# Two gated cross-attention layers on one core: in layer one ScalarE writes the masked keys, and the work of a turn is put in a new order

## The reference

```python
x = x + tanh(g_xattn[0]) * L0_xattn(layernorm(x), ctx, ctx, ...)
x = x + tanh(g_ffn[0])   * L0_ffn(layernorm(x), ...)      # 8 experts, one per token
x = x + tanh(g_xattn[1]) * L1_xattn(layernorm(x), ctx, ctx, pad_mask, ...)
x = x + tanh(g_ffn[1])   * L1_ffn(layernorm(x), ...)      # 16 dense experts

def L0_xattn(query, key, value, ...):                     # 16 heads of 8 dimensions
    q = (query @ Wq + bq).reshape(b, s, 16, 8)
    k = (key @ Wk + bk).reshape(b, s, 16, 8)
    v = (value @ Wv + bv).reshape(b, s, 16, 8)
    scores = einsum('bqhd,bkhd->bhqk', q, k) / sqrt(8)
    scores = where(k_pos < (q_pos // 32 + 1) * 32, scores, -1e9)
    return einsum('bhqk,bkhd->bqhd', softmax(scores), v) @ Wo + bo
```

## Time and profile before

| | us |
|---|---|
| three timed runs | 1631.96, 1639.06, 1639.1 (median 1639.06) |
| the profiled execution | 1626.43 |
| its span, first to last instruction | 1624.7 |
| granted TensorE clock, mean over the span | 0.981 |

### The profile page before, as it was taken

One profiled execution on the slowest core, in us unless ns is written; L12 is line 12 of the kernel. 1 busy time (PEld: TensorE's weight loads), 2 busy tenths in 40 slices (PEclk: granted clock), 3 DMA queues, 4 the chain that ended last, 5 costly groups with the idle time before them and its releaser, 6 DMA issues.

```text
span 1624.7 us, 52801 instructions
## 1 busy us (share of the span) xinstructions
PE 1513.6 (93%) x17129; PEld 1308.8 (81%) x17130; DVE 1293.3 (80%) x4044; ACT 1064.2 (65%) x2661; POOL 1186.9 (73%) x1715
## 2 busy tenths in 40 slices
PE   5899999976999789999999999999999999999996
PEld 4666666755999469888888888888888888889885
DVE  3777778863555378998999889988998999988885
ACT  3777777743556456767766776677667766776664
POOL 4556666642456568888888888888888888888785
PEclk9999999986999999999999999999999999999998
DMA  2322222234553100000000000000000000000000
GB/s 78 110 72 74 78 78 78 78 102 120 147 140 91 29 16 15 20 16 15 21 19 17 15 21 15 21 15 21 15 21 15 17 19 21 15 15 18 5 8 11
DMA packets 92108, 69.05 MB, mean 42 GB/s; under 512 B 13937, under 2 KB 87697, under 8 KB 91921
## 3 DMA queue, kind: packets, MB, share of 16 engines
q1 hardware_dynamic: 76512, 49.34, 10.3%
q0 software_dynamic: 5120, 12.62, 2.4%
q10 hardware_dynamic: 10288, 4.74, 1.1%
HBM read 35.74 MB, written 22.52 MB: 36 GB/s over the span
## 4 chain that ended last, share of the span: by engine, by line
PE 79%; issue 7%; DVE 6%; ACT 3%; DMA 2%; POOL 2%; SPq 1%; POOLq 0%; ACTq 0%; DVEq 0%
PE s_bank L1998 12%; PE s_bank L1999 11%; PE s_bank L2000 11%; PE tb L1815 6%; PE po L1945 4%; PE s_bank L1933 4%; PE s_bank L1795 4%; PE po L1829 3%; PE m L1769 2%; PE s_bank L2146 2%; PE s_bank L1804 2%; ACT pT L889 1%; DVE qkv L1552 1%; DMA kx<-kT 1%; PE s_bank L2133 1%
## 5 line engine op out<-in xcount | busy, mean ns | idle before, releaser
L745 POOL TENSOR_TENSOR qkv<-qkv,scaled 128x384 f32<-128x384 f32 x480 | 489.4, 1020 | 87.2 <-ACT scaled L1020 37.8
L1020 ACT ACTIVATE scaled<-s_bank,wg 128x384 f32<-128x384 f32 x449 | 260.3, 584 | 114.5 <-PE s_bank L2000 109.9
L1998 PE MATMUL s_bank<-proj_hi,hn_hi 128*128 128x384 f32 x900 | 327.0, 363 | 5.6 <-DVE qkv L1552 5.6
L1552 DVE SCALAR_TENSOR_TENSOR qkv<-s_bank,wg,qkv 128x384 f32<-128x384 f32 x449 | 273.9, 610 | 49.8 <-PE s_bank L2000 39.6
L1999 PE MATMUL s_bank<-proj_lo,hn_hi 128*128 128x384 f32 x900 | 302.9, 337 | 0.0
L2000 PE MATMUL s_bank<-proj_hi,hn_lo 128*128 128x384 f32 x900 | 302.2, 336 | 0.0
L889 ACT ACTIVATE pT<-tb 128x512 f32<-128x512 f32 x256 | 152.9, 597 | 136.1 <-PE tb L1815 134.5
L1998 PEld LDWEIGHTS s_bank<-proj_hi,hn_hi 128*128 128x128 f32 x900 | 169.4, 188 | 18.9 <-DVE qkv L1552 14.1
L1815 PE MATMUL tb<-ident,prob 128*128 128x128 f32 x1024 | 161.4, 281 | 15.2 <-ACT pT L889 13.8
L1999 PEld LDWEIGHTS s_bank<-proj_lo,hn_hi 128*128 128x128 f32 x900 | 170.2, 189 | 1.6
L2000 PEld LDWEIGHTS s_bank<-proj_hi,hn_lo 128*128 128x128 f32 x900 | 169.0, 188 | 0.0
(11 more groups left out here) (285 smaller groups left out, 3714.3 us busy)
## 6 DMA issues: line engine op xcount, KB each, us to landing
xs<-sorted_in SPq DMA_DIRECT2D x71, 128.5 KB, 2.1
kx<-kT SPq DMA_DIRECT2D x256, 32.0 KB
sorted_out<-yo SPq DMA_DIRECT2D x71, 64.0 KB, 1.6
xin<-in_x SPq DMA_DIRECT2D x32, 128.0 KB, 2.1
cin<-in_ctx SPq DMA_DIRECT2D x32, 128.0 KB, 2.3
ctx_cols<-xcT SPq DMA_DIRECT2D x32, 128.0 KB, 1.7
w<-in_L_ffn_W SPq DMA_DIRECT2D x16, 256.0 KB, 3.8
xcT<-ctx_cols SPq DMA_DIRECT2D x32, 128.0 KB, 2.8
```

What stands on the lines that cost most here:

```text
L745: g.tensor_tensor(into, into, scaled[m % SCALED][:, 0:cols], ALU.add).then_inc(dense_added, 1)
L1020: ins = act.activation(into, bank[:, 0:3 * D], ACT.Copy, scale=wg[v % 4][:, 1, k:k + 1])
L1552: v.scalar_tensor_tensor(out=acc, in0=bank[:, 0:3 * D], scalar=wg[w % 4][:, 0, k:k + 1], in1=acc, op0=ALU.mult, op1=ALU.add).then_inc(dens ...
L1998: pe.matmul(bank[:, 0:cols], hi[:, tile], of(proj_hi), start=True, stop=False)
```

## The change

- **Masked keys on ScalarE.** `place_keys` and `keys` are no longer used in layer one (layer two keeps them). `head_keys` reads the keys of m1 four times and writes kx[:, r, :] whole, each time with a scale column `head_mask[:, r]` (one in the partitions with p mod 4 = r, zero elsewhere) and a bias column `head_bias[:, r]` (the key bias times that mask). The two columns are made once at the start by VectorE. `k_ready` now counts two a unit, and TensorE's products wait for it in place of `keys_placed`.
- **ScalarE's turn.** exp of quad 0 before the last copy of probabilities; the four key writes and the queries before the copy of x1T; exp of quad 1 behind them; exps in the order 0, 1, 3, 2.
- **VectorE's turn.** `first_rows` a turn earlier, before the last maximum; `router_logits` ahead of `return_heads`; `router_onehot` ahead of `add_residual`; `second_rows` ahead of the first maximum; the second maximum ahead of `router_select`. `output_bias` is prepared one turn earlier.
- **TensorE's turn.** It begins with `scores`; `output(0, u)` closes the turn (the same place as before, since it stood first in the turn after). `router_rank` comes before `transpose_probs` of quad 2, `subtract_max` of quad 0 before `transpose_probs` of quad 3, and `subtract_max` of quad 3 before `transpose_probs` of quad 0.

```diff
+            def head_keys(v, pair):
+                q = s[0]
+                if exists(v):
+                    act.wait_ge(q["qk_in_psum"], v + 1)
+                    wait(act, q["scores_in_psum"], 4 * v)
+                    for r in (2 * pair, 2 * pair + 1):
+                        ins = act.activation(kx[:, r, :], m1[:, 256:512], ACT.Identity,
+                                             bias=head_bias[:, r:r + 1], scale=head_mask[:, r:r + 1])
+                    ins.then_inc(q["k_ready"], 1)
...
             def body0(u, par):
                 q = s[0]
+                exp_quad(q, u + 1, 0)
                 copy_pT(q, u, 3)
-                exp_quad(q, u + 1, 0)
                 apply_second_norm(0, u - 1, lambda t: xr[1 - par][:, t, 0:D], lambda t: xr[1 - par][:, t, D:2 * D])
+                head_keys(u + 2, 1)
+                head_keys(u + 2, 0)
+                queries(0, u + 2)
+                copy_x1T(u - 1)
                 exp_quad(q, u + 1, 1)
-                queries(0, u + 2)
-                keys(0, u + 2)
-                copy_x1T(u - 1)
-                exp_quad(q, u + 1, 2)
                 copy_pT(q, u + 1, 0)
                 exp_quad(q, u + 1, 3)
+                exp_quad(q, u + 1, 2)
                 copy_v(q, u + 2, par)
...
+            v.tensor_reduce(head_mask[:, :], ident[:, :].rearrange("p (m r) -> p r m", r=4), AX_X, ALU.add)
...
+            v.tensor_scalar(head_bias[:, :], head_mask[:, :], bcol[:, 1:2], None, ALU.mult)\
+                .then_inc(setup["first_steps"], 1)
...
                 if exists(u + 2):
                     store_context(u + 2, par)
-                    place_keys(0, u + 2)
...
                     pe.wait_ge(q["qk_ready"], v + 1)
-                    pe.wait_ge(q["keys_placed"], 64 * (v + 1))
+                    if q is s[0]:
+                        pe.wait_ge(q["k_ready"], 2 * v + 2)
+                    else:
+                        pe.wait_ge(q["keys_placed"], 64 * (v + 1))
...
-                output(0, u - 1)
                 scores(0, u + 1, 1 - par)
+                router_rank(u - 2)
                 transpose_probs(q, u, 2)
-                router_rank(u - 2)
                 transpose_in(0, u + 2, par)
+                subtract_max(q, u + 1, 0)
                 transpose_probs(q, u, 3)
-                subtract_max(q, u + 1, 0)
...
                 transpose_probs(q, u + 1, 1)
+                output(0, u)
```

More of the change, by code:

```diff
@@ L33 @@
 LOWER_MAXIMA = (0, 1, 3, 2)
-LOWER_SUBTRACTED = (0, 1, 2, 3)
+LOWER_SUBTRACTED = (0, 1, 3, 2)
 SLOTS = N // P + E0 - 1
@@ L162, in flamingo @@
         kx = sb("kx", [P, 4, UNIT])
+        head_mask = sb("head_mask", [P, 4])
+        head_bias = sb("head_bias", [P, 4])
         vb = [sb(f"vb{b}", [P, 4, 8, 2, VW]) for b in range(2)]
@@ L417, in load_unit, with place_keys @@
                 sp.dma_start(cin[par][:, :, :], tokens(a["ctx_1024"], v)).then_inc(ctx_loaded[0][par], 16)
-            def place_keys(layer, v):
-                q = s[layer]
+            def place_keys(v):
+                q = s[1]
                 sp.wait_ge(q["k_ready"], v + 1)
-                if layer == 1 and v == 1:
+                if v == 1:
                     sp.wait_ge(q["scores_in_psum"], 4)
@@ L512, in _ @@
                 load_slot(sl, sl, rows[sl] if sl < 2 else row_of(sl))
-            place_keys(1, 0)
+            place_keys(0)
             slots(sp, slot)
@@ L524, in body1 @@
                 if exists(u + 3):
-                    place_keys(1, u + 3)
+                    place_keys(u + 3)
                 store(u - 2)
             load_context(2)
-            place_keys(1, 1)
+            place_keys(1)
             load_context(3)
-            place_keys(1, 2)
+            place_keys(2)
             load_context(4)
@@ L806, in _ @@
             act.activation(sgate[:, :], sgate[:, :], ACT.Exp, scale=-1.0).then_inc(setup["scalar"], 1)
-            act.wait_ge(setup["first_steps"], 3)
+            act.wait_ge(setup["first_steps"], 4)
             def copy_xcT(v, par):
@@ L827, in keys @@
                 if exists(v):
-                    if layer == 1 and v < 2:
+                    if v < 2:
                         act.wait_ge(f["first_keys"], v + 1)
@@ L1317, in body0 @@
                 q = s[0]
-                first_rows(0, u + 2, par)
                 first_join(0, u + 2)
@@ L1322, in body0 @@
                 divide_heads(q, u - 1)
+                router_logits(u - 2)
                 return_heads(q, u - 1)
-                router_logits(u - 2)
                 router_top(u - 2)
                 router_choice(u - 2)
+                router_onehot(u - 2)
                 if exists(u - 1):
@@ L1336, in body0 @@
                 router_sum(u - 2)
+                max_quad(q, u + 1, 1)
                 router_select(u - 2)
@@ L1339, in body0 @@
                 router_row(u - 2)
-                max_quad(q, u + 1, 1)
+                router_place(u - 2, par)
                 max_quad(q, u + 1, 3)
-                router_place(u - 2, par)
+                first_rows(0, u + 3, 1 - par)
                 max_quad(q, u + 1, 2)
@@ L1345, in body0 @@
                     upper_weights()
-                if isinstance(u, int) and u == -1:
                     output_bias()
@@ L1744, in queries_keys @@
                     if layer == 0:
-                        wait(pe, q["k_ready"], v)
+                        wait(pe, q["k_ready"], 2 * v)
                         since((v - 4, route["rank_steps"], 6 * (v - 4) + 2), (v - 3, q["x_mid_ready"], v - 2),
@@ L1777, in scores @@
                     for j in range(QUADS):
-                        wait(pe, q["exp_ready"], 4 * v - 3 + j)
+                        wait(pe, q["exp_ready"], 4 * v - 3 + LOWER_SUBTRACTED.index(j))
                         quad = slice(32 * j, 32 * j + 32)
@@ L1809, in transpose_probs @@
                     if q is s[0]:
-                        pe.wait_ge(q["exp_ready"], 4 * u + j + 1)
+                        pe.wait_ge(q["exp_ready"], 4 * u + LOWER_SUBTRACTED.index(j) + 1)
                     wait(pe, q["probT_ready"], 4 * u + j)
```

8 lines of the change are left out of this document (4 added, 4 removed).

## The result

The change makes the kernel slower: 1647.48 us in the median of 8 runs against 1633.33 for the kernel before on the same chip, ratio 1.0078 with a 95% interval of 1.0056 to 1.0101. Forecast were 1614 us, with a range of 1598 to 1636 and a chance of 0.11 for slower. The key DMAs are gone as planned; a wait that the forecast didn't have in this place took over. One of the six of a later kernel, place_last, took 5039 us, for which no run gives a reason; its median isn't moved by it.

What follows compares the result with a forecast made beforehand. The prediction took a loop of waits through the key DMAs to bound the first stage's turns (10.30 us). Terms of −25.3 against the profiled 1626.43 gave 1601.1, plus 12.6 for the median: 1614 us, range 1598 to 1636.

Steps and rivals of the forecast that it cites:

- The old loop: First stage: key DMAs close the loop in nearly every turn of 10.30 us, 3.83 from kT's end to products.
- The price of a key write: ScalarE: 0.47 us from start to start, between 0.36 and 0.57; four are 1.88 a turn.
- The new loop: From x1T's end through TensorE and ScalarE's norm, four key writes and queries back to x1T: 9.7 us a turn.
- VectorE (8.26) and GpSimd have room: Step on the other engines' load a turn: VectorE 8.26 us busy, GpSimd 6.3, early statistics cost nothing.
- The unexplained pause: TensorE breaks off inside the values, 0.54 us idle, logits taken 1.36 late; costs nothing today, rivals put it on the loop.
- The rival's turn: Slower rival: the pause stays whole on the loop, 1.36 us more a turn, 11.06, total 1650; chance 0.12.
- The ends: Terms outside the 25 turns: early turns −3.7 and −1.1, late turn −2.0, first key placement −1.5, clock −2.5, start +0.5.
- The regained clock: Stretch behind the late turn at clock 0.50: full clock expected without the DMA wait, −2.5 us.
- The sum: All terms against the profiled 1626.43 us: together −25.3, of which 25 turns from 10.30 to 9.7 give −15.0.
- The 12.6 added for the median: Shown runs' median lies 12.6 us above the profiled one, so 1601.1 became 1613.7.
- the forecast's own lower end: Whole kernel: 1604 us, from 27 turns at −0.33 each, a key write at 0.36.
- the 0.36 case: Rival: key writes at 0.36 us, TensorE's busy 9.37 then bounds the turn, total 1605; chance 0.08.

Runs made afterwards that it cites:

- place_last: place_late with router_place one step later on VectorE, behind the next unit's first statistics; 1614.95 us against 1638.73 for the kernel before, ratio 0.9855.
- order_last: place_last with the keys placed by DMA again instead of written by ScalarE; 1615.98 us against 1633.50 for the kernel before, ratio 0.9902.
- place_late: The changed kernel with router_place on VectorE behind the maximum of quad 3 instead of ahead; 1602.98 us against 1623.15 for the kernel before, ratio 0.9877.
- plain_rows: The changed kernel with the same 256 rows a turn written by two plain DMAs to consecutive rows, no indirect DMA; only first stage read, turn 9.61 us.
- exp1_back: place_late with exp of quad 1 on ScalarE ahead of the key writes again, not behind x1T; one run, 1655.54 us.
- order_only: The changed kernel with keys placed by the four DMAs again, all new orders kept; 1646.98 us against 1630.61 for the kernel before, ratio 1.0073.
- order_late: order_only with router_place behind the maximum of quad 3, as in place_late; ratio 1.0213 to the kernel before.
- wait_weigh: The changed kernel with GpSimd's scatter waiting until the weighted values are in PSUM; 1628.00 us, ratio 1.0030 to the kernel before.
- place_again: place_late's program word for word on another chip; 1641.90 us against 1638.73 for the kernel before, ratio 1.0021.

## Why the prediction was wrong

- **The old loop** was misread. The late turn is as it was read: there the products wait for the key DMAs, and it fell from 11.69 to 10.99. In the 25 ordinary turns TensorE waits for them in two, 0.9 us in all, and for nothing shown in 24, inside the values:

```profile
PE s_bank L1795 <- DMA kx<-kT: 0.9, 2, 0.8
PE m L1769 <- issue: 12.5, 24, 0.6
```

  The chain that ended last, taken from 204 to 230 us, runs through TensorE's own work, one copy of probabilities a turn, and that pause, 0.52 to 0.54 each time. So neither "key DMAs close the loop in nearly every turn" nor, of the pause, "Today it lies beside the key DMA and costs nothing" fits the trace: transfer and TensorE's work ended nearly together, and only the second was the loop. order_last says the same: it has the key DMAs and a turn of 9.97, place_last's.
- **The price of a key write** was right: 0.577 us long and 1.80 for four (220.63 to 222.43), 0.45 each against 0.47. The Trainium skill (ScalarE: Activation LUTs, "What ACT_TABLE_LOAD costs") gives the terms of an estimate of 0.585; the trace has 577 ns, so it holds here.

```profile
L845 ACT ACTIVATE kx<-m,head_bias,head_mask 128x256 f32<-128x256 f32 x100 | 48.4, 577 | 0.0
```

- **The new loop** was right in number where the scatter is out of it: 9.7 forecast, 9.67 in place_late, 9.61 in plain_rows. TensorE's only wait in place_late's 25 turns is for x1T, 15.9 us, as forecast. Which step closes this loop was not tested, since exp1_back fell back into the block. In the changed kernel itself the second and third turn, before any scatter, took 8.96 and 9.64 us.
- **The step that failed** is "VectorE (8.26) and GpSimd have room; the statistics that are a turn early cost nothing". The loads were right. But in VectorE's new order `router_place` also stands ahead of the maximum of quad 3, and that of quad 1 has gone ahead of it too; the list of the change doesn't name this. The scatter needs only this row number and GpSimd free, which in the turn shown end 0.14 us apart. So it starts 1.0 us earlier against the block (0.23 behind its start in place of 1.23), opens three gaps in it and stretches it from 0.87 to 3.14. The shift was never walked through: the earlier trace rows show neither the scatter nor the block.
- **The unexplained pause** was seen, linked to the scatter and made a rival, but tied to its old place: "In the new loop logits and values are on the path", priced at one pause of 1.36. That pause did go. Values that break off are found in before, and no more in the ordinary turns of any kernel with ScalarE keys and a whole block, not even in place_last, where they start 1.8 us behind the scatter as in before (1.75). order_last, which has key DMAs and scatter, pauses 2.2 us behind the scatter's start, before 2.4; before's early turns have key DMAs and no scatter, and no pause. So that pause seems to need both, and "with the key DMAs gone, the queues near it hold far less" was borne out for it. The gaps in the weighted values need only the scatter, as order_only and the changed kernel show side by side. The block grew by 2.27, the turn over place_late's by 1.35, so 0.9 was hidden. The rival's turn, 11.06, and its 1650 us come near the measured 11.02 and 1647 by luck: a price taken from the logits' late report in another place.
- **The ends**: of the −10.3 forecast outside the 25 turns, the late turn brought −0.7 in place of −2.0, the first products came 0.2 later and not 1.0 earlier, and the stretch from them to 72 us was 0.6 longer and not 4.8 shorter: its first turn took 11.9 us, and from 54 us on the scatter is in it. The regained clock was to bring −2.5. Right behind the late turn the clock is indeed 0.96 (359.34 to 369.00) where before had 0.50, but from there to the first slot's load it took 0.8 longer, 41.4 against 40.6 us; from 372 to 384 us the clock is 0.50, with TensorE busy 6.44 of 12.
- **The sum**: in place of 25 x (9.7 − 10.30) = −15.0 stands 25 x (11.02 − 10.30) = +18.0. That term alone is 33 of the 48 us between forecast and profile (1648.86 − 1601.1). The 12.6 added for the median didn't hold either: over all runs before's median lies 6.9 above its profiled execution, the changed kernel's 1.4 below. The other sums come out as written; the forecast's own lower end, 1604, is by its terms 1604.8, the same as the 1605 of the 0.36 case.

## What to carry to other kernels

Read the loop from ordinary turns and from who waits in them; a late turn can close over another step. An idle time that waits for nothing shown is not a constant of its place. Find which other engine's instruction it follows, and when an order changes, walk that pair as one walks a wait. When a list of steps on one engine is reordered, follow each moved step to all it releases on other engines, queues too: here a row number that came 1 us earlier broke up a block on an engine that doesn't read it. And a gain measured at a distance of a few tenths of a microsecond from such a meeting should be measured on a second chip before it is believed.

## What the runs showed of the hardware

- Two indirect DMAs of 128 rows made on GpSimd, 1.09 and 0.98 us long, stretch 64 small matmuls from 0.87 to 3.14 us if they start 0.23 us behind the first of them. One makes it 1.81, and two plain DMAs of the same bytes, also made on GpSimd, leave 0.87. In place_late eight matmuls of transposes and subtractions start 0.49 to 1.33 us behind the scatter's start (199.83 to 200.67) and show no such gap.
- The gaps keep their time from the indirect DMA's start (0.65, 1.4, 2.1 us) when 2 or 8 matmuls are put ahead. At a distance of 0.5 to 0.6 a shorter one of 0.4 appears 0.2 behind it.
- Behind a block broken in this way the granted clock can fall to the lower level for some 3.5 us (order_late, 0.53), which makes that turn 1.4 us longer.
- What TensorE lacks in the gaps isn't settled. It isn't instructions that are still on their way by DMA: from 80 to 340 us of the changed kernel the DMA view has no packet of the instruction queues. A nearer shortage of instructions while GpSimd makes the DMA is a guess that no run tests.
- Open too are why the values stay whole 1.5 us behind the scatter in wait_weigh and 1.8 behind it in place_last, which the theory in its plain form doesn't say; and why one program held the edge on one chip (place_late) and not on another (place_again), while order_late broke on the first chip at the same distance.
